# Attention block of a fused transformer layer: who adds the relative-key sums, and which queue carries the maximum rows and the zero fills

## The reference, cut to what matters

```python
xn = layernorm(x)                                   # x: 4 x 1024 x 256
# attention, 16 heads of 16 channels, window W = 4
q = shape((xn @ Wq + bq) * D ** -0.5); k = shape(xn @ Wk + bk); v = shape(xn @ Wv + bv)
scores = einsum('btd,bsd->bts', q, k)
scores += rel_to_abs(einsum('btd,md->btm', q, rel_k))     # only |t - s| <= 4 is non-zero
probs = softmax(scores)
attn = einsum('bts,bsd->btd', probs, v) + abs_to_rel(probs) @ rel_v
# experts: 8, the top 2 of each token
ffn = sum over e of combine[t, e] * ((silu(xn @ w1[e]) * (xn @ w3[e])) @ w2[e])
out = x + attn @ Wo + bo + ffn
```

## Time and profile before

| | us |
|---|---|
| median of 3 runs | 2143.64 (2141.66 to 2147.24) |
| the profiled execution | 2146.0 |
| its span in the trace | 2144.1 |
| attention, from the trace | 196 to 1245 |

### The profile page before, as it was taken

How to read it: one execution, slowest core, us unless ns; L and a number is a source line. 1 busy time by engine, 2 the same in 40 slices (tenths; PEclk the granted TensorE clock), 3 DMA queues, 4 the chain that set the end, 5 groups by cost and what they waited for, 6 DMA issues and landing times. The chain is left out here.

```text
span 2144.1 us, 36132 instructions
## 1 busy us (share of the span) xinstructions
PE 1800.1 (84%) x11121; PEld 1026.0 (48%) x11121; DVE 1506.6 (70%) x2627; ACT 1103.0 (51%) x2115; POOL 773.5 (36%) x529
## 2 busy tenths in 40 slices
PE   6992328888888889899988859999999999999992
PEld 4761002222222223233322227777777777778882
DVE  3765677666666667777766239888888888898552
ACT  3541005565666566566688854444445454445550
POOL 1002899755444544400000013534444354443111
PEclk9985559999999999999999979999999999999996
DMA  5998997555543344233455156776767677675655
GB/s 181 344 347 269 250 295 208 156 134 138 143 128 104 104 137 101 77 79 69 110 165 176 40 202 224 228 228 214 247 210 237 211 231 232 212 251 168 201 166 166
DMA packets 227567, 395.56 MB, mean 184 GB/s; under 512 B 15440, under 2 KB 161760, under 8 KB 219296
## 3 DMA queue, kind: packets, MB, share of 16 engines
q1 hardware_dynamic: 193088, 279.97, 43.5%
q0 software_dynamic: 25824, 93.73, 14.3%
q10 hardware_dynamic: 8576, 20.97, 2.7%
HBM read 306.37 MB, written 87.99 MB: 184 GB/s over the span
## 5 line engine op out<-in xcount | busy, mean ns | idle before, releaser
L736 DVE CUSTOM_DVE_ANT_0 t_seen<-t_s,hide 128x1024 bf16<-128x1024 f32 x512 | 603.4, 1221 | 285.8 <-PE t_s L623 282.4
L804 ACT ACTIVATE t_pr<-t_s 128x512 f32<-128x512 f32 x1024 | 560.6, 604 | 329.2 <-PE t_s L636 231.5
L632 PE MATMUL t_s<-t_q,t_k 98*128 98x512 bf16 x1024 | 366.2, 392 | 95.6 <-DMA t_q<-t_mt 63.6
L623 PE MATMUL t_s<-t_k,t_q 96*128 96x512 bf16 x1024 | 331.5, 407 | 97.5 <-DVE t_mx L736 71.7
L1349 ACT ACTIVATE e_sg<-e_pa,e_down 128x256 f32<-128x256 f32 x312 | 148.0, 474 | 424.5 <-PE e_pa L1224 412.4
L1420 DVE SCALAR_TENSOR_TENSOR e_wl<-e_ws,e_up,e_wh 128x512 f16<-128x512 f32 x312 | 320.0, 1038 | 13.6 <-ACT e_wh L1310 0.5
L1233 PE MATMUL e_py<-e_w2s,e_hT 128*128 128x256 f32 x1248 | 324.3, 383 | 1.0 <-DVE e_hT L1442 1.0
L632 PEld LDWEIGHTS t_s<-t_q,t_k 98*128 98x128 bf16 x1024 | 97.8, 98 | 437.4 <-ACT t_pr L804 260.5
L1224 PE MATMUL e_pa<-e_xh,e_wh 128*128 128x256 f16 x1248 | 239.4, 274 | 49.0 <-DVE e_xl L1412 41.9
L647 PE MATMUL t_po<-t_pr,t_vx 128*32 128x512 f32 x2048 | 279.7, 619 | 0.7 <-ACT t_pr L804 0.7
L1224 PE MATMUL e_pa<-e_xh,e_wl 128*128 128x256 f16 x1248 | 238.7, 273 | 0.0
(11 more groups left out here) (202 smaller groups left out, 1857.5 us busy)
## 6 DMA issues: line engine op xcount, KB each, us to landing
e_ws<-in_L_ffn_w_dram SPq DMA_DIRECT2D x78, 1024.0 KB, 4.9
e_w2s<-in_L_ffn_w_dram SPq DMA_DIRECT2D x39, 1024.0 KB
e_vs<-v_rows POOLq DMA_DIRECT2D x32, 1152.0 KB, 5.8
t_kw<-k_rows POOLq DMA_DIRECT2D x22, 1152.0 KB
t_q<-q_stack SPq DMA_DIRECT2D x32, 768.0 KB, 6.1
t_k<-k_stack SPq DMA_DIRECT2D x32, 768.0 KB, 9.0
t_kw<-in_L_ffn_w_dram ACTq DMA_DIRECT2D x16, 1024.0 KB, 4.9
t_kw<-k_rows SPq DMA_DIRECT2D x10, 1152.0 KB, 7.3
```

The lines of the kernel that those rows point to most:

```text
L623: last = nc.tensor.matmul(s1[:, buf, half * CH:(half + 1) * CH], q1[0:ROWS, u, h, i * P:(i + 1) * P], k1[0:ROWS, u, h, half * CH:(half + 1 ...
L632: last = nc.tensor.matmul(s2[:, bank, :], k2[0:ROWS + MROWS, u, h, i * P:(i + 1) * P], q2[0:ROWS + MROWS, u, h, half * CH:(half + 1) * CH] ...
L736: nc.vector.tensor_tensor_reduce(out=seen[:, buf, :], in0=s1[:, buf, :], in1=c["hide"][:, (TB - 1 - i) * P:(TB - 1 - i) * P + L], scale=1. ...
L804: nc.scalar.activation(pr[:, k % BP, n % HG], s2[:, turn(u, n)], ACT.Exp).then_inc(exp_ok, 1)
```

## The change

- GpSimd adds `dot` to `band` itself, right after the last halving of a window, waits for its own sum before it and for the addition before it goes on; `dot` has one buffer. It no longer waits for VectorE.
- VectorE only takes the maximum over the nine. For group 0 it does all 32 pass 1 tiles first and then the eight windows of batch 0.
- ScalarE issues the maximum rows on its own queue, right after it has copied them, and waits for its own copy first. SP no longer does, nor waits for it.
- The 13 zero fills and the fill of `expert_sums` leave SP's queue. ScalarE issues all 14 behind the maximum rows of group 0 and ahead of its first exp.

```diff
-        dot = sb("dot", [P, 2, NM * H])
+        dot = sb("dot", [P, NM * H])
...
-                sp.wait_ge(zero_ok, 2)
                 for t in range(2, TB + 2):
                     sp.wait_ge(sum_ok, t - 1)
                     load_window(sp, t, t % 2, win_early)
-                    for z in range((t - 2) * N_ZERO // TB, (t - 1) * N_ZERO // TB):
-                        sp.dma_start(zeros[z], zero[:].broadcast_to([P, 6, XE])).then_inc(zero_out, 16)
-                sums = dr["moe"].rearrange("(n p) e -> p n e", p=P)
-                sp.dma_start(sums, zero[:, :, 0:E].broadcast_to([P, NT + 1, E])).then_inc(sums_out, 16)
-                maximum(0, 0)
                 load2(1, 0, 1, 1)
...
-                    maximum(g + 1, 1 - u)
...
-                            after(pool, band_ok, t - 1)
-                            nc.gpsimd.tensor_tensor(dot[:, u, :].rearrange("p (q o) -> p q o", o=1), terms[:, :, 0:w],
+                            nc.gpsimd.tensor_tensor(dot[:].rearrange("p (q o) -> p q o", o=1), terms[:, :, 0:w],
                                                     terms[:, :, w:2 * w], ALU.add).then_inc(sum_ok, 1)
+                    pool.wait_ge(sum_ok, t + 1)
+                    scores = band[:, t, :, :].rearrange("p m h -> p (m h)")
+                    nc.gpsimd.tensor_tensor(scores, scores, dot[:], ALU.add).then_inc(band_ok, 1)
                     if more:
-                        pool.wait_ge(sum_ok, t + 1)
                         load_window(pool, t + 2, u, win_in)
+                    pool.wait_ge(band_ok, t + 1)
...
-                        if g0 and n % HG >= HG - PIECES:
-                            window(n // HG, n // HG % 2, n % HG - (HG - PIECES))
-                        elif more and not g0 and n in range(8, 8 + 2 * PIECES, 2):
-                            window(TB * (b + 1) + 2 * v, 0, (n - 8) // 2)
+                        if more and not g0 and n == 8:
+                            window(TB * (b + 1) + 2 * v)
...
+                    if g0:
+                        for t in range(TB):
+                            window(t)
...
-                def keep_maximum(g):
+                def keep_maximum(g, u):
                     act.wait_ge(mt_ps_ok, g + 1)
                     after(act, m_in, 16 * MROWS * g)
                     nc.scalar.copy(mt[:], s1[0:2 * HG * TB, 0, 0:P // 2].bitcast(BF16)).then_inc(mt_ok, 1)
+                    act.wait_ge(mt_ok, g + 1)
+                    for j in range(MROWS):
+                        act.dma_start(q2[ROWS + j:ROWS + j + 1, u].rearrange("o h (i t) -> o (h i) t", t=P),
+                                      mt[j * HG * TB:(j + 1) * HG * TB, :]).then_inc(m_in, 16)
...
-                keep_maximum(0)
+                keep_maximum(0, 0)
+                zeros = dr["xs"].rearrange("(z r p) e -> z p r e", p=P, r=6)
+                act.wait_ge(zero_ok, 2)
+                for z in range(N_ZERO):
+                    act.dma_start(zeros[z], zero[:].broadcast_to([P, 6, XE])).then_inc(zero_out, 16)
+                sums = dr["moe"].rearrange("(n p) e -> p n e", p=P)
+                act.dma_start(sums, zero[:, :, 0:E].broadcast_to([P, NT + 1, E])).then_inc(sums_out, 16)
                 exps(0, 0)
```

More of the change, by code:

```diff
@@ L408, in attention @@
     XS = 2 * TB * HG
-    PIECES, FOLDS = 2, 4
+    FOLDS = 4
     HF = XS // X
@@ L501, in load2 @@
                     sp.dma_start(vx[:, u], vd[b, gg]).then_inc(vin[u], 16)
[L503 to L509, removed]
                 load1(0, 0)
@@ L548, in _ @@
                 step(14, 0, 0, 0, more1=False, more2=False)
-                sp.wait_ge(sums_out, 16)
             @block.gpsimd
@@ L708, in _, with window @@
                 neg_v = neg[:].rearrange("p (b i) (g h) -> p b g h i", i=TB, h=HG)
[L710 to L720, removed]
+                def window(t):
+                    dve.wait_ge(band_ok, t + 1)
+                    nc.vector.tensor_reduce(bmax[:, t, :], band[:, t, :, :].rearrange("p m h -> p h m"),
+                                            AX.X, ALU.max).then_inc(bmax_ok, 1)
                 def maxima(b, v):
@@ L747, in maxima @@
                     if g0:
-                        for piece in range(PIECES):
-                            window(TB, 0, piece)
+                        window(TB)
                     if more:
-                        for piece in range(PIECES):
-                            window(TB * (b + 1) + 2 * v + 1, 1, piece)
+                        window(TB * (b + 1) + 2 * v + 1)
                 nc.vector.memset(mparts[:], 0.0).then_inc(zeros_ok, 1)
@@ L813, in exps @@
                         if n == XS - MLEAD + 1 and not (isinstance(b, int) and g == NG - 1):
-                            keep_maximum(g + 1)
+                            keep_maximum(g + 1, 1 - u)
                         if isinstance(b, int) and b == NB - 1:
@@ L834, in _ @@
                 keep_rows(NB - 1, final, 1)
+                act.wait_ge(sums_out, 16)
 def route(nc, block, ctx, logits, logits_ok, psum, dst, meta, spare, table, iota_e, slot_expert):
```

## The result

| | us |
|---|---|
| before, 4 runs beside the changed kernel | 2145.44 (2141.66 to 2148.57) |
| changed, 4 runs | 2169.44 (2167.54 to 2173.75) |
| ratio | 1.0115, 95% interval 1.0091 to 1.014 |
| the profiled execution of the changed kernel | 2167.5, its span 2165.8 |

The change makes the kernel 1.15% slower, some 24 us. 2151.6 with a range of 2126 to 2182 was predicted: slower was the likeliest side and the range holds the time, but the forecast is 18 us too low. Chips differ a little: beside the experiments the kernel before took 2136 to 2140 us. Experiments 1 to 4 and 9 to 11 ran on one chip and 5 to 8 on another, and the changed kernel itself was not run on the first, so kernels from different chips are compared by their ratios alone.

The account below looks back on a forecast made before the run. It took TensorE's waits in attention, the largest for maximum rows (63.6 us), as the bound. Ninth tile +46, clock +2, boundaries -52 and ports +12 gave +8 us: 2151.6 us, range 2126 to 2182.

Parts of the forecast that it names:

- The sum: Whole kernel: 46 + 2 - 52 + 12 = +8 us on the profiled execution of 2146.0 us.
- I am wrong if: Test: fills landing before 345 or after 365 us, or TensorE's maximum-row waits staying above 20 us in sum.
- other signs: First send near 355, ninth tile near 384, no later row wait over 1 us, groups 52 to 55 us apart.
- The ninth tile, +46: Start of group 1: windows wait behind a send for the late fills; VectorE's ninth tile at 384, not 338.23: 46 us lost.
- ScalarE's hold: Start: the fill issues hold ScalarE to 351 or so, costing nothing because TensorE waits for VectorE until 368.
- The maxima of group 0, nothing: Start: group 0's maximum rows issued at 311.8 us, 2.2 us later than before; nothing gained.
- The boundaries, -52: Group boundaries: rows on ScalarE's queue let TensorE start 5.4 us behind the copy, 6.1 us saved at nine; 52 us together.
- ScalarE's loss of 0.9 us: Each boundary: ScalarE's two issues and its wait for its own copy delay its exps by 0.9 us (0.3 to 1.4).
- The ports, +12: Seven boundaries: GpSimd's work holds VectorE's small operations, 1.7 us lost at each; 12 us (0 to 60).
- the rival's: Rival of biting ports: each held operation frees the next into GpSimd's next one; +42 instead of 12, 2182 us, chance 0.16.
- GpSimd done near 720 us: GpSimd, no longer waiting for VectorE, makes 21 windows after the tenth at 16 us each, to about 720 us.
- The rival of rows that land no earlier: Boundaries: DMA engines stay busy with the same loads, 9 us stay 9, only the 48 us delay remains; 2192, chance 0.10.

Follow-up runs that it names:

- experiment 1: Changed kernel with the zero fills issued by SP again, paced between its first window loads; 2122.68 us, ratio 0.9935 to the kernel before.
- experiment 2: Kernel before with only ScalarE issuing the maximum rows behind its copy; 2133.89 us, ratio 0.9984.
- experiment 3: Kernel before with only GpSimd adding its sums to the band, rows and fills on SP; 2119.08 us, ratio 0.9908.
- experiment 4: Changed kernel with GpSimd's sends of tiles beginning at window 12 instead of window 8; 2147.15 us, ratio 1.0054 to the kernel before.
- experiment 9: Kernel before with SP issuing the maximum rows ahead of load1 instead of behind it; 2119.63 us, ratio 0.9908.
- experiment 10: Changed kernel, fills on ScalarE, with GpSimd's window loads from window 12 on waiting for the maximum rows; 2135.13 us, ratio 0.9979 to the kernel before.
- experiment 11: Experiment 7's kernel with only group 0's rows issued by ScalarE and sends starting at window 11; 2081.75 us, ratio 0.9729 to the kernel before.
- experiment 5: Changed kernel run again without an edit, on another chip; 2163.58 us, ratio 1.0115 to the kernel before.
- experiment 6: Experiment 1's kernel with GpSimd's window loads from window 12 on waiting until the maximum rows have landed; 2092.86 us, ratio 0.9775 to the kernel before.
- experiment 7: Experiment 3's kernel with experiment 6's load wait, and SP issuing the maximum rows ahead of load1; 2084.35 us, ratio 0.9744 to the kernel before.
- experiment 8: Kernel before run again without an edit, for a profile from another chip; one execution, 2144.47 us.

## Why the prediction was near, and where it was off

The sum was +8 us. The profiled execution is 21.7 us longer than that of the kernel before: 48.4 us lost by the first boundary (48 were foretold), 28.2 given back by the last copy of the maxima (1217.72 against 1197.54 us, 20.2), and 1.5 more to the end. The prediction said "I am wrong if" TensorE's wait for the maximum rows "stays above 20 us in sum". It is 25.7 us, 10.1 of them for group 0, so by its own test the prediction was wrong about the boundaries. Of its other signs, no later boundary was to wait over 1 us, and four waited 2.8 to 4.5; groups were to be 52 to 55 us apart, and up to the fifth boundary they are 58.7. That the time still lies in the range is in part luck: the gain that came at the boundaries came by another way and later than the one forecast.

- **The ninth tile, +46.** Right, 3 us low: window 10 at 387.3 where 384 was said, and 44 us (39 to 49) by experiment 10. The `send` was the binding wait, and ScalarE's hold the next one, hidden (experiment 4). The fills had landed by 358.7, when the first `send` starts, and not by 355; in the profiles of experiments 5 and 10 it starts at 353.6 and 355.2, and window 10 is there at 382.2 and 383.7.
- **The maxima of group 0, nothing.** Right: issue at 312.38 for 311.8.
- **The boundaries, -52.** This is the step that failed. The words were: the rows leave ScalarE's queue, "where nothing lies ahead", and "have 3.9 us to land". At the first five boundaries they had company on the DMA engines and TensorE started 7.8 to 9.5 us behind the copy where it waited. The changed kernel gave back 28.2 us; boundaries and ports together were put at 40. Some 24 us of that came after the fifth boundary (44.7 us there), when GpSimd was nearly through with its loads; nine boundaries of 6.1 us from the first on were foretold.
- **The reading behind it.** I set beside the earlier trace rows and took `load1` and the two issues on SP's queue for the cause of 9.05 against 4.48 us. What tells them apart was in the rows too: GpSimd's load at 434.99 stands in the earlier trace rows and none does in the earlier trace rows. The queue was the same in both. Experiments 2, 3 and 9 show it: another queue saves 3 us, and without a window load the wait is about 1 us even on SP. `load1` ahead of the rows has a smaller share: some 2 us of the landing (4.6 to 5.9 us in experiment 6, 3.0 in experiment 7).
- **Where the rows landed in time,** 5.4 us behind the copy was right (5.46), ScalarE's loss of 0.9 us too as far as it can be told (some 1 us by experiments 1 and 7). Experiment 7, where a group lasts 52.0 us at a clock of 1.00 while GpSimd works, also shows that the clock comes back once the waits are gone.
- **The ports, +12.** Of the right order, and uneven: TensorE's waits for the small operations after group 0, before any loss of clock, sum up to 5.6 us in the profile of the changed kernel, to 4.5 in experiment 5, 13.6 in experiment 1 and 15.1 in experiment 4. Where they were held longest the rows were there in time (the boundaries at 547 and 720 us), so not all of it comes on top. In shape it was the rival's: when the first is held, the next start inside GpSimd's next operations.

```profile
536.84 5.07 POOL L552 TENSOR_TENSOR t_kw<-t_kw,t_qw 128x2304 f32<-128x2304 f32 x1
541.30 0.69 DVE L723 TENSOR_TENSOR t_mb<-t_mx,bmax 128x32 f32<-128x32 f32 x1
541.99 4.87 POOL L558 TENSOR_TENSOR t_kw<-t_kw 128x1152 f32<-128x1152 f32 x3
542.02 2.61 DVE L724 TENSOR_SCALAR t_mparts<-t_mb 128x32 bf16<-128x32 f32 x1
...
544.90 1.28 DVE L727 TENSOR_TENSOR neg<-t_mparts 128x32 f32<-128x32 bf16 x1
...
546.23 0.23 PE L649 MATMUL t_s<-ident,t_mparts 128*128 128x128 bf16 x1 [2.70 <-DVE neg L727]
```

- **GpSimd done near 720 us** was right (the last addition to the band is at 720.42, the last load at 692), and mattered more than I gave it: I used it for the ports alone, and it also decides from where the rows land in time.
- **The rest.** From the last copy to the end the kernel before took 946.6 us and the changed one 948.1; all kernels here lie between 946.2 and 948.8, whatever was changed, so these 1.5 us are scatter.
- **The rival of rows that land no earlier** (2192) was right on its cause while GpSimd loads windows, and wrong after that. The rule it named, of the Trainium skill, "DMA: Bandwidth & Descriptors", section "Rules for kernel authors", says that spreading over issuing engines brings no bandwidth; it says nothing of when a small transfer lands. For the time of this kernel experiment 2 agrees with 0.9984, and group 0's rows, 16.6 us of wait against 8.9, are the case where a queue of their own did count.

By parts, as ratios to the kernel before: the rows on ScalarE -3 us (experiment 2), the band on GpSimd -20 (experiment 3), both -14 (experiment 1), the fills +38 to +44 on top (experiments 1 and 10). Why both are less than their sum was not tried apart; experiment 1's profile has 7 us more of waits for the small operations than experiment 3's (13.6 against 6.4), and ScalarE's 1 us a group buys little once GpSimd's loads are over.

## What to carry to other kernels

When a small transfer lands late, look at what large transfers were issued shortly before it on any queue, and not only at its own: set a late case beside one in time and list every DMA that differs. A cheap remedy is to let the large load wait for the small one (here 34 us of 2140). A bulk transfer whose place is free should not begin right ahead of a wait for all of it, and when work is moved to an engine that then runs free, ask what the others' periodic work will meet there.

## What the runs showed of the hardware that I had not expected

- Two 8 KB transfers land 3.0 us behind the copy when they are issued ahead of the large ones (experiment 7), and 4.6 to 5.9 us behind it on ScalarE's queue when `load1`, of 1.5 MB, was issued on SP's 4.7 us before the copy (experiment 6). They let TensorE start only 6.4 to 8.8 us behind it if a window load was issued 1.3 us before the copy, though nothing was ahead of them on their own queue (experiment 9). In these runs a load issued shortly before them counts against them on another queue as well.
- 14 fills behind each other held ScalarE for 38 us, from 313.7 to 351.7 us; a single issue took up to 12.4 us.
- Of four small VectorE operations of 0.2 us in a row three were held beside GpSimd's operations: 4.65, 2.60, 0.19 and 1.28 us, for group 0, the same in every kernel in which GpSimd adds to the band.
